# A transformer layer on one core: who multiplies the rounded 704-wide row by its scales

## The reference

```python
def fp4_quant_dequant(x):
    xb = x.reshape(shape[:-1] + (shape[-1] // BLOCK, BLOCK))      # BLOCK = 16
    scale = jnp.max(jnp.abs(xb), axis=-1, keepdims=True) / 6.0
    scale = jnp.maximum(scale, jnp.float32(1e-12))
    xn = xb / scale
    idx = jnp.searchsorted(_MID, jnp.abs(xn))
    q = _GRID[idx] * jnp.sign(xn) * scale
    return q.reshape(shape)
...
gate = fp4_linear(x, w_gate)
y = fp4_linear(x, w_up)
h = jax.nn.silu(gate) * y                                         # 704 wide
return fp4_linear(h, w_down)
```

## Time and profile before

| what | value |
|---|---|
| median of 3 runs | 2490.33 us (2486.07 to 2491.36) |
| profiled execution, its time | 2487.88 us |
| profiled execution, its span | 2486.2 us |
| PE busy over the span | 2349.4 us, 95% |
| DVE busy over the span | 1910.8 us, 77% |
| ACT busy over the span | 1432.6 us, 58% |
| POOL busy over the span | 607.1 us, 24% |
| the 32 executions of L1283 on POOL | 44.4 us together |

### The profile page before, as it was taken

How to read it: one execution, slowest core, us unless ns; L and a number is a source line. 1 busy time by engine, 2 the same in 40 slices (tenths; PEclk the granted TensorE clock), 3 DMA queues, 4 the chain that set the end, 5 groups by cost and what they waited for, 6 DMA issues and landing times. The chain is left out here.

```text
span 2486.2 us, 48992 instructions
## 1 busy us (share of the span) xinstructions
PE 2349.4 (95%) x19372; PEld 1168.7 (47%) x19372; DVE 1910.8 (77%) x3509; ACT 1432.6 (58%) x2724; POOL 607.1 (24%) x361
## 2 busy tenths in 40 slices
PE   7899999999999999999999999999999974899997
PEld 3424444444444444444444444444444433666665
DVE  6687777777777777777777777777777707999997
ACT  3416666666666666666666666666666651434432
POOL 5402233222222222222223322222222220111111
PEclk9959999999999999999999999999999995999999
DMA  5733323332334333333323332333332211111110
GB/s 156 200 82 87 88 84 88 88 88 85 109 96 106 95 89 88 89 87 94 89 80 93 88 88 80 92 106 100 95 94 84 74 34 41 41 42 51 42 44 26
DMA packets 275666, 210.43 MB, mean 85 GB/s; under 512 B 17058, under 2 KB 266628, under 8 KB 275332
## 3 DMA queue, kind: packets, MB, share of 16 engines
q1 hardware_dynamic: 274308, 203.37, 30.0%
q0 software_dynamic: 1152, 4.19, 0.6%
HBM read 113.35 MB, written 93.34 MB: 83 GB/s over the span
## 5 line engine op out<-in xcount | busy, mean ns | idle before, releaser
L1049 DVE TENSOR_REDUCE amax<-psA 128x1 f32<-128x512 f32 x2048 | 1312.8, 684 | 407.0 <-PE psA L758 395.4
L1019 ACT ACTIVATE probs<-psS 128x512 f32<-128x512 f32 x1792 | 927.9, 609 | 411.2 <-PE psS L868 411.2
L758 PE MATMUL psA<-keys,queries 96*128 96x512 bf16 x2048 | 771.9, 390 | 1.6 <-DVE amax L1049 1.6
L868 PE MATMUL psS<-queries,keys 102*128 102x512 bf16 (+7 forms) x2176 | 637.5, 344 | 18.9 <-ACT probs L1019 4.1
L784 PE MATMUL psC<-probs,vals 128*32 128x512 f32 (+7 forms) x4352 | 475.0, 524 | 0.1
L719 POOL TENSOR_TENSOR band_probs<-band_probs,side 128x2048 f32<-128x2048 f32 x64 | 288.7, 4533 | 514.2 <-PE psC L880 514.2
L868 PEld LDWEIGHTS psS<-queries,keys 102*128 102x128 bf16 (+1 forms) x2176 | 195.8, 98 | 355.1 <-ACT probs L1019 157.4
L758 PEld LDWEIGHTS psA<-keys,queries 96*128 96x128 bf16 x2048 | 195.7, 97 | 345.5 <-DVE amax L1049 269.1
L1014 ACT ACTIVATE band_probs<-psS 128x512 f32<-128x512 f32 x256 | 153.0, 598 | 152.5 <-PE psS L857 152.3
L998 ACT COPY rel_scores<-psS 128x512 f32<-128x512 f32 x256 | 137.2, 590 | 72.8 <-PE psS L772 72.8
L784 PEld LDWEIGHTS psC<-probs,vals 128*32 128x32 f32 (+1 forms) x4352 | 89.1, 102 | 167.4 <-issue 86.1
(11 more groups left out here) (162 smaller groups left out, 2056.9 us busy)
## 6 DMA issues: line engine op xcount, KB each, us to landing
rel_skew<-rel_scores SPq DMA_DIRECT2D x32, 2048.0 KB, 7.6
rel_near<-rel_skew SPq DMA_DIRECT2D x64, 1024.0 KB, 8.2
keys<-k_ring SPq DMA_DIRECT2D x48, 256.0 KB, 5.8
queries<-q_parts SPq DMA_DIRECT2D x192, 64.0 KB, 2.4
ctx_d<-rden SPq DMA_DIRECT2D x32, 256.0 KB, 2.3
ctx_in<-ctx_d SPq DMA_DIRECT2D x32, 256.0 KB, 2.7
q_parts<-parts SPq DMA_DIRECT2D x16, 384.0 KB, 3.0
k_ring<-parts SPq DMA_DIRECT2D x12, 384.0 KB, 3.3
```

The costliest lines, as they stand in the source:

```text
L758: t.matmul(psA[:, (first + n) % ABANKS, :], qs[0:NR, qb, h, u * P:(u + 1) * P], keys[0:NR, par, h, c0:c0 + NQ], start=True, stop=True).the ...
L868: ins = t.matmul(bank[:, o:o + k], keys[0:nr, par, h, c0:c0 + P], qs[0:nr, qb, h, q0:q0 + k], start=True, stop=True, skip_group_check=True)
L1019: ins = a.activation(probs[:, n % 4, half], src, ACT.Exp)
L1049: v.reduce_max(amax[:, pair, k:k + 1], psA[:, (first + n) % ABANKS, :], AX.X).then_inc(max_taken, 1)
```

## The change

VectorE issues the multiplication by the scales as an eleventh instruction of the H chain, and GpSimd's program in this part is gone. In `DVE_ORDER` the H of the subtraction now stands three X earlier, and the new multiplication takes the place that the subtraction had, the last before Y. Y waits for the multiplication (`hq_ready`) and no longer for the subtraction.

```diff
-        DVE_ORDER = "HXHXHXHXHHHXXHXXHXXXXXXXXHY"
+        DVE_ORDER = "HXHXHXHXHHHXXHXXHXXXXXHXXXHY"
...
-        @block.gpsimd
-        def _(pool):
-            def scale_hidden(n, k):
-
-                pool.wait_ge(hs_ready, n + 1)
-                nc.gpsimd.tensor_tensor(hq[:, k].rearrange("p (b k) -> p b k", k=QBLK), hs[:, k].rearrange("p (b k) -> p b k", k=QBLK),
-                                        hsc[:, k, :, None].broadcast_to([P, FFN // QBLK, QBLK]), ALU.mult).then_inc(hq_ready, 1)
-
-            def step(n, r, left, some):
-                scale_hidden(n, r % 2)
-
-            pipeline(pool, step)
...
                 v.tensor_sub(hs[:, k], tmp[:], bits[:]).then_inc(hs_ready, 1)
+                yield
+                dve.wait_ge(hs_ready, n + 1)
+                v.tensor_tensor(hq[:, k].rearrange("p (b k) -> p b k", k=QBLK), hs[:, k].rearrange("p (b k) -> p b k", k=QBLK),
+                                hsc[:, k, :, None].broadcast_to([P, FFN // QBLK, QBLK]), ALU.mult).then_inc(hq_ready, 1)
...
-                        dve.wait_ge(hs_ready, n + 1)
+                        dve.wait_ge(hq_ready, n + 1)
```

## The result

The changed kernel takes 2508.28 us (median of 6 runs, 2507.28 to 2509.62), the kernel before 2488.85 us (6 runs, 2486.07 to 2491.36). The ratio is 1.0079, with a 95% interval of 1.0066 to 1.0092. The forecast was 2508.5 us in a range of 2503 to 2515. In a second comparison on one chip the changed kernel took 2507.06 us against 2487.29, ratio 1.0081 (1.0068 to 1.0095).

A forecast was written before the change was run, and what follows sets the result against it. VectorE was taken to bound the step, with TensorE 0.9 us behind. Thirty steps at 0.70 us (21.0) minus 2.0 at the end made 19.0 us more, so 2508.5 us, in a range of 2503 to 2515.

The forecast's parts named there:

- VectorE sets the step: Feed-forward loop: VectorE, busy 10.66 of 11.44 us a step, bounds it; TensorE follows with 0.9 us to spare.
- The step grows by 0.70 us: End of VectorE's step: distances between starts make 0.22 + 0.81 - 0.33 = 0.70 us more; bounds 0.60 and 0.92.
- the rival that nothing overlaps: VectorE's step: grows by the full 0.92 us, 25.6 us in all, so 2513.5 to 2516 us; chance 10%.
- The rule against the overlap: VectorE: the skill's DRAIN rule, next instruction starts only once the pipe empties; a step would grow by 0.92 us.
- Thirty steps, 21.0 us: Steps 0 to 29, which have the X chain: 30 ends of a step grow by 0.70 us, 21.0 us.
- The end gives back 2.0 us: Steps 29 and 31: turn_h no longer waits through GpSimd, saving 1.46 + 0.53 us, about 2.0.
- The forecast's 19.0: Whole kernel: 21.0 us from the steps minus 2.0 from the end.
- 2506.9 and 2509.3: Whole kernel: forecast time from the profiled execution's 2487.88 us and from the runs' median 2490.33; 2508.5 named between them.
- TensorE is freer: TensorE in the loop: idles 1.7 us a step instead of 1.0, waiting for VectorE's f_xq and f_hq.
- GpSimd's removal gives nothing back: VectorE beside GpSimd: L1506 takes 886 to 889 ns in all executions, so removing GpSimd's work counts 0.
- The clock: TensorE in the loop: granted clock stays 1.00; rival that it falls puts the time near 2680 us; chance 3%.

The follow-up runs named there:

- GpSimd late: The changed kernel with GpSimd also multiplying each tile, into a tile nobody reads, started behind VectorE's multiplication; 2506.67 us, ratio 1.0081.
- early table load: The kernel before, with ScalarE loading its square-root table before the copies of f_hq instead of behind them; 2487.18 us, ratio 0.9995.

## Why the prediction was right

**VectorE sets the step.** Right, and now shown from both sides: one more 0.89 us instruction on VectorE lengthens the step by 0.78 us, some 1.0 us more on TensorE by 0.04.

**The step grows by 0.70 us.** Measured 0.71. The parts were 0.22, 0.81, 0.92, 0.34, 1.08 in the forecast and 0.20, 0.81, 0.91, 0.34, 1.08 in the trace. The run with the subtraction put back separates this from the rival that nothing overlaps. That the sum came out so close is in part luck. An ordinary step grew by 0.67 us, from 11.38 to 12.05: its parts make 3.34 where the forecast had 3.37. The average reaches 0.71 because the second step of each round of the loop is another 0.11 us longer: there Y starts 1.18 us behind the multiplication's start (1.43 in the first round), where the kernel before has 1.08 from the subtraction to Y. The second step of two rounds of the changed kernel, VectorE alone:

```profile
2147.33 0.88 DVE L1502 TENSOR_TENSOR f_hq<-f_h_grid,f_h_scale 128x704 f32<-128x704 f32 x1
2148.76 0.42 DVE L1512 TENSOR_TENSOR f_y<-psD,x 128x256 f32<-128x256 f32 x1 [0.54 <-DVE f_hq L1502]
...
2196.27 0.88 DVE L1502 TENSOR_TENSOR f_hq<-f_h_grid,f_h_scale 128x704 f32<-128x704 f32 x1
2197.45 0.42 DVE L1512 TENSOR_TENSOR f_y<-psD,x 128x256 f32<-128x256 f32 x1 [0.30 <-DVE f_hq L1502]
```

The second profile of this kernel has the same distances, and so have the runs with the subtraction put back and with more on TensorE; those with two multiplications and with GpSimd late have 1.08 there. No run shows why.

**The rule against the overlap.** I had cut it short. The same section of "VectorE: DVE Perf Modes" in the Trainium skill goes on that a next instruction that isn't held starts earlier. The starts 0.08 us before the recorded end agree with that; so the skill doesn't speak for the rival that nothing overlaps.

**Thirty steps, 21.0 us.** The profiled executions have 30 x 0.71 = 21.3.

**The end gives back 2.0 us.** The sign is right, the size is not: 1.25 us. `turn_h` comes earlier by what was forecast. In step 29 it starts 0.44 us ahead of the next L1493, where it started 1.03 behind the next L1506, so 1.47 us are saved; in step 31 it starts 1.87 us behind the subtraction's start instead of 2.41, so 0.54. But of the 1.47 only 0.71 reach `gate_up`. It now waits for L1493 and starts 1.03 us behind it, where it started 1.74 behind L1506 (2456.18 to 2457.92). The lines of TensorE in the end, first of the kernel before (the others of it are in the earlier trace rows):

```profile
2456.18 0.89 DVE L1506 TENSOR_TENSOR f_silu<-f_silu,psG 128x704 f32<-128x704 f32 x1
...
2478.51 4.90 PE L1376 MATMUL psD<-w_down_T,f_hqT 128*128 128x256 f32 x12 [0.99 <-ACT f_hqT L1404]
```

Then of the changed kernel, whose L1493 of step 30 is at 2477.12, with the busy times of the same stretches:

```profile
2476.68 0.88 PE L1354 MATMUL psH<-ident,f_hq 128*128 128x128 f32 x6 [0.36 <-DVE f_hq L1502]
2478.15 7.99 PE L1331 MATMUL psG<-w_gate_up_T,f_xqT 128*128 128x352 f32 x16 [0.59 <-DVE f_silu L1493]
...
2497.07 0.88 PE L1354 MATMUL psH<-ident,f_hq 128*128 128x128 f32 x6 [3.30 <-DVE f_hq L1502]
2498.94 5.78 PE L1363 MATMUL psD<-w_down_T,f_hqT 128*128 128x256 f32 x12 [0.99 <-ACT f_hqT L1391]
```

```profile
2478.15:2486.14 7.99, 7.99 (x17) 4.86 (x18) 6.20 (x10) 0.35 (x3) 0.00 (x0) 0.62 0.04 12
...
2498.94:2504.72 5.78, 5.78 (x12) 3.69 (x12) 0.00 (x0) 0.00 (x0) 0.00 (x0) 0.50 0.02 4
```

And of the changed kernel once more:

```profile
2478.22 6.18 PE L1331 MATMUL psG<-w_gate_up_T,f_xqT 128*128 128x352 f32 x16 [0.36 <-DVE f_silu L1493]
...
2495.33 1.54 PE L1354 MATMUL psH<-ident,f_hq 128*128 128x128 f32 x6 [3.30 <-DVE f_hq L1502]
2497.87 4.65 PE L1363 MATMUL psD<-w_down_T,f_hqT 128*128 128x256 f32 x12 [0.99 <-ACT f_hqT L1391]
```

```profile
2478.22:2484.40 6.18, 6.18 (x17) 3.92 (x18) 5.87 (x10) 0.59 (x3) 0.00 (x0) 0.80 0.05 16
2497.87:2502.52 4.65, 4.65 (x12) 3.26 (x12) 0.00 (x0) 0.00 (x0) 0.00 (x0) 0.65 0.01 2
```

The stretches have their granted clock as the third number from the end: 0.62 and 0.50 in the one, 0.80 and 0.65 in the other (0.50 is the 1.2 GHz level throughout). This clock hides the saving. The end takes 27.7 us in the one profile and 25.4 in the other, and 27.3 and 25.3 in those of the kernel before and of the one with the early table load. Without the durations of `gate_up` of tile 31 and of `turn_h` and the last down projection in step 31, which go with the clock, it is 27.33 - 6.59 - 1.54 - 4.90 = 14.30 us before (14.29 with the early table load) and 27.70 - 7.99 - 0.88 - 5.78 = 13.05 after, and 25.42 - 6.18 - 1.54 - 4.65 = 13.05 in the second profile.

**The time.** The steps and the end make 21.3 - 1.25 = 20.1 us; the medians differ by 19.4 and 19.8, and the clock of the end alone can move an execution by 2. The forecast's 19.0 is 1.1 below 20.1, 0.3 by the steps and 0.75 by the end. That 2508.5 lies 0.2 us from the measured 2508.28 is luck: it was picked between 2506.9 and 2509.3.

**TensorE is freer.** Right in direction, too large, and wrong in the parts. Its recorded idle time rose from 0.98 us a step to 1.22, not to 1.7. I foresaw waits for `f_xq` and `f_hq` and overlooked that `gate_up` also waits until silu times up has read PSUM. With `turn_h` no longer behind GpSimd, it comes before that instruction's end, and 0.8 us of the wait moved there. In the loop this costs nothing, since it is slack; at the end it took some 0.75 us from the saving.

**GpSimd's removal gives nothing back.** Right for this order, on too narrow a ground. I had read that three instructions beside GpSimd keep their durations, and had not said why: they each have an operand in PSUM. With two SBUF operands beside it the step pays 1.07 us. The same section of "GPSIMD Engine Reference" in the Trainium skill, set against the rows, would have warned that the early subtraction and the multiplication on GpSimd may not go together. That run had this only as a rival, and the rival is what came.

**The clock.** 1.00 in the loop, as forecast; it moves only the end.

## What to carry to other kernels

On a full VectorE count distances between starts, not durations: here an instruction whose neighbour belongs to another chain cost 0.08 us less than its duration, a dependent one 0.03 more than it; and where a separate wait for the instruction just in front is issued, as at Y, the next started 0.19 us behind its end. When work moves off an engine, ask what order it had forced: the new order may be worth as much as the move costs. And when VectorE gets shorter, look for the next ring before counting the gain: here it was ScalarE's table load, then Y's wait for TensorE, only 0.03 us a step behind it. And where an end phase runs at a changing clock, compare it without the pieces that the clock stretches.

## What the runs showed of the hardware

A 256-wide TENSOR_TENSOR of VectorE with two SBUF operands that came to start while a GpSimd TENSOR_TENSOR was running took 1491 ns instead of 425, in all 30 cases, in two kernels; GpSimd's own instruction, which had started during the preceding VectorE instruction, took 1.50 us instead of 1.39. In the two steps without an X chain GpSimd's instruction started 0.04 us behind VectorE's L1513, which is 0.89 us long and has two SBUF operands: there L1513 kept its duration, and GpSimd's took 2.09 us. So in these runs the one that started second was the one held up. Instructions of VectorE with one PSUM operand kept their durations to within 3 ns beside the same GpSimd instruction. TensorE's end phase varied by 2.3 us between two executions of one kernel, with `gate_up` at 7.99 and 6.18 us, at a granted clock of 0.62 and 0.80, where it took 4.90 at a clock of 1.00. VectorE's f32 TENSOR_TENSOR took 0.88 to 0.89 us for 704 elements and 0.42 to 0.43 for 256. The next instruction started 0.81 or 0.34 us after its start when it didn't wait for it, and 0.92 or 0.46 us when it did.
